# Token order, the path of the values and the placing of the expert tiles in a fused attention and expert kernel

## What is computed

```python
x = L0_attn_x                                   # 16 x 256 x 128, fp32
xn = _layernorm(x, axis=-1)
s = _L0_attn_ref(xn, ...)                       # 16 heads of 8, q/k/v with a rank-8 addition,
                                                # slopes * (i - j), causal mask, softmax, @ Wp.T
g = _silu(_L0_ffn_ref(xn, ...))                 # 8 experts, 128 -> 512 -> 128, one expert per token
x = x + s * g

# in _L0_ffn_ref, for each expert i
mask = (indices == i).astype(x.dtype)[..., None]
h = jax.nn.relu((x * mask) @ W1[i] + b1[i])
out = out + (h @ W2[i] + b2[i])
```

## Time and profile before

| | |
|---|---|
| median of 3 runs | 415.79 us (415.49 to 418.18) |
| the profiled execution | 416.0 us |
| its span, first to last instruction | 413.8 us |
| mean granted clock of TensorE | 0.901 |
| busy: TensorE, its weight loads | 361.2 us, 249.6 us |
| busy: VectorE, ScalarE, GpSimd | 214.9 us, 218.0 us, 109.9 us |

### The profile page before, as it was taken

The page is one execution under the profiler, slowest core; times in us unless marked ns, Lnnn a source line. Parts: engine busy times, 40 slices in busy tenths (PEclk is TensorE's granted clock), DMA queues, the critical chain, the costliest instruction groups (busy, mean ns, idle before and its releaser), DMA issues.

```text
span 413.8 us, 12674 instructions
## 1 busy us (share of the span) xinstructions
PE 361.2 (87%) x5178; PEld 249.6 (60%) x5178; DVE 214.9 (52%) x483; ACT 218.0 (53%) x381; POOL 109.9 (27%) x113
## 2 busy tenths in 40 slices
PE   6799599996899898998989989899899667679993
PEld 2589465573577675776757767576665334445551
DVE  4821798624355555554455555555554654785201
ACT  1367016542475665665657666566645445446661
POOL 2202173786011100111001111011114558773200
PEclk9655589998699999998999999999999696898996
DMA  7996559553132223321424132332315324521100
GB/s 220 225 274 204 202 181 399 178 159 122 50 99 76 92 82 109 99 90 40 114 90 118 59 96 78 103 99 63 97 53 161 96 76 129 154 74 31 29 27 27
DMA packets 58920, 48.39 MB, mean 117 GB/s; under 512 B 4584, under 2 KB 53352, under 8 KB 58864
## 3 DMA queue, kind: packets, MB, share of 16 engines
q1 hardware_dynamic: 56816, 43.39, 34.5%
q0 software_dynamic: 2048, 4.20, 3.6%
HBM read 25.29 MB, written 21.89 MB: 114 GB/s over the span
## 4 chain that ended last, share of the span: by engine, by line
PE 70%; DVE 9%; POOL 7%; issue 6%; ACT 4%; DMA 4%; DVEq 0%; ACTq 0%; POOLq 0%
PE bank L998 12%; PE bank L1049 11%; PE bank L1098 9%; PE bank L1106 8%; PE bank L928 7%; POOL sorted_rows L452 5%; PE bank L1006 5%; PE bank L942 3%; PE bank L1082 2%; PE bank L1068 2%; PE bank L978 2%; DVE row_max L702 2%; PE bank L919 2%; ACT probs L595 1%; PE bank L1059 1%
## 5 line engine op out<-in xcount | busy, mean ns | idle before, releaser
L702 DVE TENSOR_REDUCE row_max<-bank 128x2 f32<-128x512 f32 (+3 forms) x176 | 109.7, 639 | 64.5 <-PE bank L986 64.3
L595 ACT ACTIVATE probs<-bank 128x512 f32<-128x512 f32 (+1 forms) x176 | 95.3, 557 | 64.0 <-PE bank L1006 63.6
L998 PE MATMUL bank<-q_stack,k_stack 64*64 64x64 bf16 (+3 forms) x1024 | 78.8, 267 | 13.0 <-DVE rem L674 11.3
L1049 PE MATMUL bank<-probs,v_diag 128*32 128x64 f32 (+3 forms) x1024 | 71.3, 322 | 13.1 <-ACT probs L595 12.5
L978 PE MATMUL bank<-k_stack,q_stack 54*64 54x64 bf16 (+3 forms) x1024 | 81.1, 273 | 1.1 <-DVE row_max L702 1.0
L998 PEld LDWEIGHTS bank<-q_stack,k_stack 64*64 64x64 bf16 x1024 | 46.2, 145 | 38.4 <-issue 30.6
L438 POOL TENSOR_TENSOR parts<-rem,parts 128x512 bf16<-128x512 f32 x16 | 18.5, 1158 | 148.5 <-ACT parts L522 148.5
L986 PE MATMUL bank<-cb 64*64 64x128 bf16 (+2 forms) x352 | 56.8, 319 | 0.0
L812 DVE TENSOR_TENSOR hT<-bank,w_slots 128x512 f32<-128x512 f32 x39 | 27.0, 692 | 55.0 <-PE bank L1098 55.0
L1006 PE MATMUL bank<-cb 64*64 64x128 bf16 (+2 forms) x352 | 55.0, 307 | 0.0
L1049 PEld LDWEIGHTS bank<-probs,v_diag 128*32 128x32 f32 x1024 | 23.8, 111 | 45.8 <-ACT probs L595 23.0
(11 more groups left out here) (113 smaller groups left out, 403.5 us busy)
## 6 DMA issues: line engine op xcount, KB each, us to landing
qk_parts<-parts SPq DMA_DIRECT2D x32, 192.0 KB, 2.9
q_stack<-qk_parts SPq DMA_DIRECT2D x32, 192.0 KB
k_stack<-qk_parts SPq DMA_DIRECT2D x32, 192.0 KB
qk_parts<-parts SPq DMA_DIRECT2D x32, 128.0 KB, 2.9
w_all<-w_experts SPq DMA_DIRECT2D x8, 512.0 KB, 7.8
sorted_rows<-zeros SPq DMA_DIRECT2D x1, 2496.0 KB, 11.6
expert_rows<-y_slot SPq DMA_DIRECT2D x39, 64.0 KB, 1.5
xs_slot<-sorted_rows SPq DMA_DIRECT2D x9, 256.0 KB, 3.2
```

The costliest lines, as they stand in the source:

```text
L595: act.activation(probs[:, g % PROBS, 0:w], bank[:, 0:w], ACT.Exp).then_inc(emptied, 1)
L702: dve.tensor_reduce(row_max[b % 2][:, n, pairs[0]:pairs[-1] + 1], bank[:, 0:ln_u * len(pairs)].rearrange("p (c k) -> p c k", k=ln_u), AX.X ...
L998: pe.matmul(bank[rows, c * ln_u:(c + 1) * ln_u], k[rows, p, kb::NBLK], blocks(q[rows, p, :], kb, NBLK), start=(c == 0), stop=False, skip_g ...
L1049: last = pe.matmul(by_block[:, :, kb:NBLK], v_diag[b % 2][:, kb, p, :], probs[:, (b * NU + w) % PROBS, c * ln_u:(c + 1) * ln_u], start=(kb ...
```

## The change

- Blocks of 64 are neighbouring tokens. All reads and writes that stepped by block order become runs of 64; the constants for the slopes follow.
- ScalarE writes projected values straight into `v_diag`, in two copies of half the partitions; `v_ring` and `spread_v` go, and values are projected one entry ahead instead of two.
- The expert tiles stand at every unit from unit 0 of step 4 on, to unit 6 of step 7. Rows are first loaded and turned at the last unit of step 3. Gathers begin in step 8, gates at unit 9 of step 8.
- Scatters are spread to four before the loop, nine in step 0, nine in step 1, ten in step 2. In steps with scatters or gathers `third_part` stands behind the first four of them.
- GpSimd takes half of the normalisations that ScalarE had. The zeroing of the sorted rows is three DMAs, between the stacks.
- `remainder` moves to unit 2, between `relu` and `keep_y`; `second_part` moves to unit 4.

```diff
-FIRST_PLACE = 2 * NU + 2
-PLACES = [divmod(FIRST_PLACE + 11 * t // 5, NU) for t in range(SLOT_TILES + 1)]
+FIRST_PLACE = 4 * NU
+PLACES = [divmod(FIRST_PLACE + t, NU) for t in range(SLOT_TILES + 1)]
...
-TURN_AT = {PLACES[max(4 * q - 2, 0)]: q for q in range(1, QUADS)} | {(2, 1): 0}
+ROWS_PLACE = divmod(FIRST_PLACE - 1, NU)
+TURN_AT = {PLACES[max(4 * q - 2, 0)]: q for q in range(1, QUADS)} | {ROWS_PLACE: 0}
...
-GATE_AT = {divmod(FIRST_GATHER * NU + 8 + 5 * c, NU): c for c in range(CHUNKS)}
+GATE_AT = {divmod(FIRST_GATHER * NU + 9 + 5 * c, NU): c for c in range(CHUNKS)}
...
-SCATTERED_BEFORE, SCATTERED = 10, {0: 22, 1: NT}
+SCATTERED_BEFORE, SCATTERED = 4, {0: 13, 1: 22, 2: NT}
...
@@ SyncE
+            def zero_rows(c):
+
+                tiles = slice(c * SLOT_TILES // 3, (c + 1) * SLOT_TILES // 3)
+                sp.dma_start(xs_dram.rearrange("(p r) d -> p r d", p=P)[:, tiles],
+                             zeros[:, :].unsqueeze(1).to_broadcast([P, SLOT_TILES // 3, D])).then_inc(S["zeros_out"], 16)
+
+            load_stacks(0)
             sp.wait_ge(S["zero_src"], 1)
-            sp.dma_start(xs_dram.rearrange("(p r) d -> p r d", p=P),
-                         zeros[:, :].unsqueeze(1).to_broadcast([P, SLOT_TILES, D])).then_inc(S["zeros_out"], 16)
-            load_stacks(0)
+            zero_rows(0)
             for part in range(3):
                 store_part(2, part)
             load_stacks(1)
+            zero_rows(1)
             for part in range(3):
                 store_part(3, part)
             load_stacks(2)
+            zero_rows(2)
             load_stacks(3)
...
@@ GpSimd
-            def spread_v(b):
...
+            def normalise(n):
+                pool.tensor_scalar(xn_all[:, n, :], x_all[:, n, :], rstd[:, n:n + 1], nmr[:, n:n + 1], ALU.mult, ALU.add).then_inc(S["xn_pool"], 1)
...
             third_part(0)
             third_part(1)
-            spread_v(0)
-            third_part(2)
-            third_part(3)
+            pool.wait_ge(S["nmr_done"], 2)
+            for n in range(NT // 4, NT, 2):
+                normalise(n)
+                if n in (20, 26):
+                    third_part(2 + n // 26)
             pool.wait_ge(S["slots_done"], 1)
-            pool.wait_ge(S["zeros_out"], 16)
+            pool.wait_ge(S["zeros_out"], 16 * 3)
...
             for i in range(NB):
-                if i + 1 < NB:
-                    spread_v(i + 1)
-                if i + AHEAD < NB:
+                if i in SCATTERED:
+                    n0, n1 = SCATTERED.get(i - 1, SCATTERED_BEFORE), SCATTERED[i]
+                    scatter(n0, n0 + 4)
                     third_part(i + AHEAD)
-                if i in SCATTERED:
-                    scatter(SCATTERED.get(i - 1, SCATTERED_BEFORE), SCATTERED[i])
+                    scatter(n0 + 4, n1)
+                elif i + AHEAD < NB and i not in GATHERED:
+                    third_part(i + AHEAD)
...
                 if i in GATHERED:
-                    gather(GATHERED.get(i - 1, 0), GATHERED[i])
+                    n0, n1 = GATHERED.get(i - 1, 0), GATHERED[i]
+                    gather(n0, n0 + 4)
+                    if i + AHEAD < NB:
+                        third_part(i + AHEAD)
+                    gather(n0 + 4, n1)
...
@@ ScalarE
             def keep_v(b):
-                wait(act, "vdiag_done", b - 1)
+                wait(act, "pv_ps", (b - 1) * NPV)
                 bank, emptied = wait_act_full(act, "v", b)
-                act.activation(v_ring[:, b % 2].rearrange("p n h d -> p (n h d)"), bank[:, 0:T], ACT.Copy).then_inc(emptied, 1)
+                for a in range(2):
+                    half = slice(HALF * a, HALF * (a + 1))
+                    last = act.activation(v_halves[b % 2][half, :, a, 0:DH], bank[half, 0:T].rearrange("p (c d) -> p c d", d=DH), ACT.Copy)
...
-                for n in range(4 * g, 4 * g + 4):
+                for n in (4 * g + 1, 4 * g + 3):
                     normalise(n)
...
-                        if u == PROJECT + 3:
+                        if u == PROJECT + 2:
                             second_part(i + AHEAD)
...
-                    if i + 2 < NB and u == VALUES_OF:
-                        keep_v(i + 2)
+                    if i + 1 < NB and u == VALUES_OF:
+                        keep_v(i + 1)
...
@@ VectorE
-                    if u == PROJECT + 1 and i + AHEAD < NB:
-                        remainder(i + AHEAD)
...
-                    if (i, u) in TILE_AT:
-                        t = TILE_AT[i, u]
-                        if t < SLOT_TILES:
-                            relu(t)
-                        if t > 0:
-                            keep_y(t - 1)
+                    if TILE_AT.get((i, u), SLOT_TILES) < SLOT_TILES:
+                        relu(TILE_AT[i, u])
+                    if u == PROJECT and i + AHEAD < NB:
+                        remainder(i + AHEAD)
+                    if TILE_AT.get((i, u), 0) > 0:
+                        keep_y(TILE_AT[i, u] - 1)
...
@@ TensorE
-                by_block = xnT_all[:, b, :].rearrange("p (k i) -> p i k", k=NBLK)
                 for n in range(2):
-                    last = pe.matmul(bank[:, n * T:(n + 1) * T], w_eff[:, n, :], by_block, start=(n == 0), stop=True, skip_group_check=True)
+                    last = pe.matmul(bank[:, n * T:(n + 1) * T], w_eff[:, n, :], xnT_all[:, b, :], start=(n == 0), stop=True, skip_group_check=True)
...
-                    last = pe.matmul(bank[to, 0:ln_u * len(pairs)].rearrange("p (c k) -> p c k", k=ln_u)[:, :, n::n + 1], ident_b[rows, rows],
+                    last = pe.matmul(bank[to, 0:ln_u * len(pairs)].rearrange("p (c k) -> p c k", k=ln_u)[:, :, n * BLK:], ident_b[rows, rows],
...
-                    pe.matmul(bank[rows, c * ln_u:(c + 1) * ln_u], k[rows, p, kb::NBLK], blocks(q[rows, p, :], kb, NBLK),
+                    pe.matmul(bank[rows, c * ln_u:(c + 1) * ln_u], k[rows, p, kb * BLK:(kb + 1) * BLK], q[rows, p, kb * BLK:],
...
-                        by_block = pv_bank[32 * j:32 * j + 32, g * T:(g + 1) * T].rearrange("p (k i) -> p i k", k=NBLK)
-                        last = pe.matmul(by_block[:, :, kb:NBLK], v_diag[b % 2][:, kb, p, :],
+                        last = pe.matmul(pv_bank[32 * j:32 * j + 32, g * T + kb * BLK:(g + 1) * T], v_diag[b % 2][:, kb, p, :],
...
-                    last = pe.matmul(bank[0:3 * NP, n::NBLK], nmax[b % 2][:, n].rearrange("p c h -> p (c h)"), ident_b, start=(n == 0),
-                                     stop=True, skip_group_check=True)
+                    last = pe.matmul(by_block[:, n], nmax[b % 2][:, n].rearrange("p c h -> p (c h)"),
+                                     ident_b.rearrange("p (a k) -> p a k", a=2), start=(n == 0), stop=True, skip_group_check=True)
...
             project_v(0)
-            project_v(1)
             turn(1)
...
@@ constants
-    rise = slope.reshape(NP, 2).T[:, :, None] * (np.arange(T) % NBLK * BLK + np.arange(T) // NBLK)
+    rise = slope.reshape(NP, 2).T[:, :, None] * np.arange(T)
```

More of the change, by code:

```diff
@@ L110, in bank_uses @@
         if g == 0:
-            act += [("v", 0), ("v", 1)]
+            act.append(("v", 0))
     for b in range(2):
@@ L963, in count_before @@
                 last.then_inc(S["rank_ps"], 1)
-            def blocks(columns, low, high):
-                return columns.rearrange("p (i k) -> p i k", k=NBLK)[:, :, low:high]
             def stack_ready(b):
```

44 lines of the change are left out of this document (22 added, 22 removed).

## The result

The changed kernel took 383.64 us at the median (381.66 to 385.65, 4 runs), the kernel before 415.64 (4 runs, 414.31 to 418.18, on the same chip). The ratio is 0.9224, 95% interval 0.9147 to 0.93: faster by 8%. The forecast was 370, in the range of 358 to 390, and 13.6 us too low. The hit holds for this chip: on a chip of the experiments the same change came to 0.9653 of the kernel before, and the upper end of the range, 390 beside 415.8, is 0.938.

A forecast was written before the change was run, and what follows sets the result against it. TensorE was taken to bound the loop body, with other bounds in step 2 and steps 10 to 13. Window terms summed to 368.1 us; 2.2 on top gave 370.3, forecast as 370, range 358 to 390.

The forecast's parts named there:

- Natural order in the projections: Projections in the loop: contiguous reads take 0.9 us off each of twelve, 10.8 us in all; bounds 0 and 1.05 each.
- rival 2: Projections, masks and maxima: strides are not the reason, so those gains stay away and the total is 389 us; chance 0.08.
- Masks and maxima: Mask matmuls and turn_max: natural order gains 0.8 us a step where TensorE is the bound, half in a light step.
- rival 4: Value products, counted at nothing in the forecast, gain from natural order too: 14 us, total 356 us; chance 0.04.
- The remainder a unit earlier: Tile steps: the remainder ahead of keep_y in the projection's unit removes TensorE's seven waits, 11.3 us.
- In light steps: Eight light steps with a projection: the earlier remainder delays turn_max by about 0.7 us each, 5.6 us; bounds 0 and 0.7.
- The 4.8 us wait goes: Sorted rows: scatters end by about 114, rows load at 122 in step 3, so TensorE's wait and low clock (0.84) go.
- Steps 1 and 2: Forecast lengths: step 1 20.4 us; step 2 15.4 us, including 2.0 for spreading the constant rows.
- Steps 10 and 11: GpSimd's additions, three at the head of step 10 and one in step 11, delay VectorE by 2.5 and 1.0 us.
- rival 1: Steps 10 to 13: the tail stays as costly as it was, adding 17 us for a total of 387 us; chance 0.17.
- Prologue: Before step 0: about +1.4 us from GpSimd's queued normalisations against about -1.4 from dropped work; counted 0, bounds -1.5 and +1.5.
- Rivals 3 and 5: First (0.11): light steps fare better, 360 us; second (0.03): the ring of three weight slots makes it slower than before.

The follow-up runs named there:

- Rows early: The changed kernel with the first two loads of sorted rows issued at unit 5 of step 3 instead of unit 10: 448.4 us, 0.9561 of the kernel before.

## Why the prediction was right, and where it was short

**Natural order in the projections** (0.9 each): right, 0.87 measured; so rival 2 was wrong, as rows 3 and 4 said. The matmuls themselves came out at 0.27 to 0.28 us each and not near 0.22, so the upper bound of 1.05 was out of reach. **Masks and maxima** (0.8 a tile step): right, 0.92 on the chain, masks at 0.05 and 0.10, turn_max at 0.20. A tile step gained 2.46, not 1.7, and what is missing is a term that the sum put at nothing: the score products and their weight loads, 0.71 a step, because the sum prices the strides of the fp32 operand and of PSUM and leaves out those of the bf16 queries and keys. **Values products**: nothing gained, as forecast; rival 4 is wrong, and with it the general form of the rule on PSUM patterns that the prediction takes from the Trainium skill ("SBUF — State Buffer", "Door 1"): over the whole run their matmuls are busy for 72.6 us, before for 71.3.

**The remainder a unit earlier** in tile steps: right, by itself it gave 10.8 us (0.976) for the 11.3 of the seven waits. "Late next is hidden of the following unit" was wrong as a place (that wait is 0.5 us in three). Late next was the division of the outputs, 1.0 us in each of steps 4 to 7. I had followed the banks at the old pace of tiles, not at the new one. This miss (+3.9) and the unnamed gain of the scores (0.71 to 0.76 in each of four steps, some -3) all but hide each other: that steps 4 to 7 came out at 129.7 for a forecast of 129.5 is luck. **In light steps** (0.7 each, 5.6): oversized. Of the 6.5 us that TensorE waits for nmax, 0.9 are in the prologue and 1.2 in step 13, outside these steps. Steps 0, 1, 3, 8 and 9 have 0.36 each, half of the forecast, steps 2 and 10 none over 0.15, and step 11 the 2.59 of the second hold. So the move itself cost some 1.8 us. The chain of projection, first part, remainder, unit_max, last part in step 3 (the weight load waits 0.85, the matmul behind it 0.36):
```profile
119.10 1.13 PE L940 MATMUL bank<-xnT_all,w_eff 128*128 128x256 f32 x4
...
120.95 0.69 DVE L687 TENSOR_TENSOR rem<-bank,parts 128x512 f32<-128x512 f32 x1 [0.85 <-ACT parts L524]
...
122.16 0.18 DVE L736 TENSOR_TENSOR nmax<-nmax_rem,nmax 128x32 bf16<-128x32 f32 x1
...
122.39 0.22 PEld L1068 LDWEIGHTS bank<-cb,nmax 128*24 128x24 bf16 x4 [0.85 <-DVE nmax L736]
```

**"The 4.8 us wait goes"**: this step failed. The scatters were done by 118.3, some 4 us behind the sum's 114 and still ahead of the rows' place, but I took the end of the scatters for the arrival of the rows. The loads stand at the last unit of step 3, behind SyncE's stores of parts, and TensorE turns the rows in that same unit; a transfer of 4.11 us has no cover there. It is 3.9 of step 3's 4.2, with a low clock behind it in this step and the next (0.50 from 133 to 136 and 0.69 from 136 to 140). Rows early removed both: 3.2 us of step 3 and 1.6 of step 4. So a wait of 4.8 us became one of 3.9 in another step, where the sum had none.

**Steps 1 and 2** (+2.4, +3.1): mostly clock. A mean clock of 0.93 over 22.8 us is 3.2 us at half clock, with 1.6 lost by an estimate that takes TensorE as the bound; 0.82 over 18.5 is 6.7, with 3.3 lost; before, step 1 had 1.00. In step 1 the windows show 0.59 from 78 to 81, after idle times of TensorE of 0.39, 0.30 and 0.73 from 74.6 on. In step 2 the clock falls as the last products of the constant rows (99.29 to 101.48) end:
```profile
100.00:102.00 2.00, 2.00 (x15) 0.56 (x14) 1.18 (x2) 0.00 (x0) 0.00 (x0) 0.73 0.38 131
102.00:104.00 2.00, 2.00 (x28) 1.27 (x24) 1.04 (x4) 0.62 (x2) 0.00 (x0) 0.50 0.11 33
```
TensorE had idled 0.54 us for the constant rows before 99.29; the clock then fell to 0.50 (1.2 GHz) and was back at 1.00 by 108. The kernel before does the same at the same place, with a wait of 0.46 us before these products (97.17 to 99.15):
```profile
98.00:100.00 2.00, 2.00 (x19) 0.91 (x17) 1.50 (x3) 0.27 (x1) 1.46 (x2) 0.97 0.49 188
100.00:102.00 2.00, 0.42 (x3) 0.02 (x1) 1.58 (x2) 1.49 (x2) 1.50 (x2) 0.50 0.18 59
```
There the clock is already falling before 100, and the wait of 4.8 us for the sorted rows begins only at 100.4. So the second half of "the 4.8 us wait goes, with the low clock beside it (0.84)" failed as well: the fall came ahead of that wait and not from it, and it stayed (0.82). The sum counts this step at full clock. What makes the clock fall there isn't shown: both times it follows a short idle and these products.

**Steps 10 and 11** (2.5 and 1.0): the hold in step 10 was 3.7 us, not 2.5, since three additions lie in a row at 1.24 each, and 2.5 is what two had taken. In step 11 the addition held nothing, but the third part did, 1.6 us, and TensorE waited 2.59 for it; and again the step pays in clock:
```profile
312.00:315.00 3.00, 1.64 (x33) 0.80 (x32) 2.82 (x7) 2.10 (x4) 2.39 (x3) 1.00 0.72 191
315.00:318.00 3.00, 1.49 (x28) 1.10 (x28) 2.16 (x3) 0.79 (x2) 2.80 (x4) 0.66 0.66 170
318.00:321.00 3.00, 3.00 (x42) 1.71 (x36) 1.34 (x4) 1.86 (x5) 0.82 (x1) 0.50 0.42 124
```
TensorE is half idle from 312 to 318, and from 316 on the clock is at half. A mean of 0.80 over 17.5 us is at most 3.5 lost, by the same estimate; TensorE was busy for only 14.20 of these 17.50, so the wait and the clock overlap and how step 11's miss of 3.1 divides between them isn't shown. This is rival 1's "waits feed on themselves", at 4.4 us and not at 17; the waits for gathers are gone, and it needed those in full.

**Prologue** (0, bounds -1.5 and +1.5): the third part at 33.33 held the normalisations and the transposes waited 1.40, as priced; step 0 ended 0.9 late. On the other chips the same part cost far more than its upper bound. The bound came from TensorE's waits and not from where the part moves the scatters.

**Rivals 3 and 5**: light steps came out worse than forecast, not better; the ring of weight slots decided nothing, with tile units at 34.6 / 11 = 3.15 us as forecast. Unsettled on the first chip, where only the two kernels ran: what the new places, the values and the prologue bring each by themselves.

## What to carry to other kernels

When a wait is to be removed by a later place, follow the last link (here the load behind a queue's stores) to its consumer and not just the slow link. When work is packed closer, walk the rotation of banks at the new pace: the next wait is where an emptying engine had slack only because the work was thin. And price a stall of TensorE with the low clock that may follow it: the wait of 3.9 us in step 3 cost another 1.6 in step 4, and in steps 1 and 2 the low clock stands for an estimated 1.6 and 3.3 us, behind single idle times of 0.3 to 0.7.

## What the runs showed of the hardware

With the step of four columns gone from the bf16 operands in SBUF, weight loads of 64x64 went from 144 to 106 ns and score matmuls from 263 to 237; both operands changed at once, so their shares aren't told apart. The step of 64 elements in the fp32 operand takes a projection from 1.13 to 1.93 us on the chain. Writes to PSUM in steps double a bf16 mask (0.05 to 0.10) and leave the fp32 value products as they are (0.36).

A VectorE operation of 0.17 us lasted 3.70, to the end of three additions that GpSimd ran in a row, and one of 0.18 us lasted 1.81, to the end of an indirect DMA and a third part in a row.

On the chips of the three groups the kernel before was 12 to 13% slower than on the first, the changed one 18% on the one where it ran, in the prologue and light steps with indirect DMAs alone, with TensorE in places at one or two matmuls per 0.7 us and idle on nothing that the trace names. Taking 24 of 32 gathers away gave back some 31 us. On such chips order and remainder without new places (0.9219) and the change without its values and prologue part (0.9224) stand well ahead of the whole change (0.9653). Which is best on the first chip was not tried.
